# A first selective scan in pieces of 512 columns, and a quarter of each product with C on another engine

## The reference, cut to what matters

```python
def step(state, inp):                      # state: 256 channels x 16 states, for each of 4 sequences
    d, b, c, u = inp                       # one of 256 positions
    dA = jnp.exp(d[..., None] * A)
    state = state * dA + (d * u)[..., None] * b[:, None, :]
    y = jnp.einsum('bdn,bn->bd', state, c)
    return (state, y)
_, ys = jax.lax.scan(step, state0, (dt_t, B_t, C_t, u_t))
```

## Time and profile before

| | us |
|---|---|
| median of 3 timed runs (996.51 to 998.3) | 996.89 |
| span of the profiled execution | 994.6 |
| TensorE busy | 824.6 |
| VectorE busy | 670.0 |
| POOL busy | 419.8 |
| ScalarE busy | 406.1 |
| 32 scans of the first block (L616) | 73.3 |
| 32 products with C (L625) | 38.4 |
| 32 drives (L600) | 75.4 |

### The profile page before, as it was taken

How to read it: one execution, slowest core, us unless ns; L and a number is a source line. 1 busy time by engine, 2 the same in 40 slices (tenths; PEclk the granted TensorE clock), 3 DMA queues, 4 the chain that set the end, 5 groups by cost and what they waited for, 6 DMA issues and landing times.

```text
span 994.6 us, 12963 instructions
## 1 busy us (share of the span) xinstructions
PE 824.6 (83%) x4202; PEld 523.7 (53%) x4202; DVE 670.0 (67%) x1145; ACT 406.1 (41%) x832; POOL 419.8 (42%) x313
## 2 busy tenths in 40 slices
PE   7968898756899888888399779999948988979992
PEld 3323333344677767665377535555525776546651
DVE  5989999697889888889565556778727365412222
ACT  5742333253344444443354725665523432113331
POOL 3036666113575766665169402425501341423331
PEclk9979988756999999999599889999978996979997
DMA  5121214381221221220200121332144010161114
GB/s 216 48 84 67 81 64 181 157 271 52 85 85 50 78 84 42 84 84 0 75 0 1 54 64 50 100 114 76 49 144 135 1 58 7 48 202 48 44 48 153
DMA packets 28531, 81.68 MB, mean 82 GB/s; under 512 B 3360, under 2 KB 17200, under 8 KB 27088
## 3 DMA queue, kind: packets, MB, share of 16 engines
q1 hardware_dynamic: 26080, 73.25, 21.5%
q0 software_dynamic: 2256, 6.18, 1.7%
q10 hardware_dynamic: 144, 1.57, 0.4%
HBM read 65.64 MB, written 17.35 MB: 83 GB/s over the span
## 4 chain that ended last, share of the span: by engine, by line
PE 46%; issue 21%; DVE 17%; POOL 9%; DMA 3%; ACT 2%; SPq 0%; DVEq 0%; POOLq 0%; ACTq 0%
PE ps L522 5%; POOL M L689 5%; PE ps L1357 5%; PE ps L1727 4%; PE ps L1731 4%; PE ps L513 3%; PE ps L1769 3%; PE ps L396 3%; PE ps L911 3%; POOL ZT L994 2%; DVE M L658 2%; PE ps L1376 2%; DVE M L666 2%; PE ps L799 2%; PE ps L1642 1%
## 5 line engine op out<-in xcount | busy, mean ns | idle before, releaser
L799 PE MATMUL ps<-W,F 128*128 128x256 f32 x544 | 151.9, 404 | 34.8 <-DVE W L867 21.7
L799 PEld LDWEIGHTS ps<-W,F 128*128 128x128 f32 x544 | 102.2, 198 | 67.6 <-DVE W L867 40.9
L600 POOL TENSOR_TENSOR M<-M 128x1024 f32<-128x1024 f32 x32 | 75.4, 2356 | 86.1 <-DVE M L474 47.4
L696 POOL TENSOR_TENSOR W<-W,M 128x1024 f32<-128x1024 f32 x32 | 75.4, 2357 | 84.4 <-DVE M L666 84.4
L1798 ACT ACTIVATE N<-ps 128x512 f32<-128x512 f32 x128 | 69.5, 594 | 75.7 <-PE ps L1731 75.7
L831 ACT ACTIVATE F<-ps 128x128 f32<-128x128 f32 x136 | 37.8, 278 | 140.0 <-PE ps L799 140.0
L658 DVE TENSOR_TENSOR_SCAN M<-ps,M 128x512 f32<-128x512 f32 x64 | 78.0, 1219 | 21.5 <-POOL M L689 21.5
L1819 DVE TENSOR_REDUCE W<-ps 128x4 f32<-128x1024 f32 x64 | 78.1, 1221 | 8.9 <-PE ps L1731 5.9
L786 PE MATMUL ps<-W,F 128*128 128x256 f32 x272 | 83.3, 389 | 0.0
L1727 PE MATMUL ps<-M,W 32*128 32x256 f32 x512 | 74.1, 418 | 10.8 <-DVE W L1825 5.7
L616 DVE TENSOR_TENSOR_SCAN M<-ps,M 128x1024 f32<-128x1024 f32 x32 | 73.3, 2291 | 10.3 <-ACT ps L569 10.1
(11 more groups left out here) (281 smaller groups left out, 1708.8 us busy)
## 6 DMA issues: line engine op xcount, KB each, us to landing
M<-dbl_scratch SPq DMA_DIRECT2D x48, 512.0 KB, 3.7
W<-in_gu SPq DMA_DIRECT2D x1, 4800.0 KB, 16.3
W<-in_gu SPq DMA_DIRECT2D x1, 4352.0 KB, 13.9
att_scratch<-W SPq DMA_DIRECT2D x32, 128.0 KB
slot_scratch<-in_slots SPq DMA_DIRECT2D x1, 3999.0 KB, 18.7
M<-slot_scratch SPq DMA_DIRECT2D x3, 1032.0 KB, 9.6
W<-in_gu SPq DMA_DIRECT2D x2, 1536.0 KB, 6.7
W<-in_dn SPq DMA_DIRECT2D x1, 2176.0 KB, 18.6
```

What stands on the lines that cost most here:

```text
L600: nc.gpsimd.tensor_tensor(dBu[:, t, :], du[0][:, t, :], Bb[:, par, :], ALU.mult).then_inc(S("dBu_rdy"), 1)
L696: nc.gpsimd.tensor_tensor(u[1][:, t, :], u[1][:, t, :], hC[:, t, :], ALU.add).then_inc(S("y1_acc"), 1)
L799: last = nc.tensor.matmul(up, ztt[:, par, c, :], gu[:, c, s, :], start=(c == 0), stop=(c == DC - 1))
```

## The change

- `scan` becomes two scans of 512 columns, each with a bank of decays of its own; `decays` writes 510 columns at a time and waits for the scan of that half before. `h_rdy` now counts four a state. ScalarE's loop over the states is written out.
- VectorE's product covers columns 0 to 767 (`OWN`). Columns 768 to 1023 are made by POOL (`weigh_rest`, L611 after) from the state in SBUF and `Cb`, into which SP loads the last 256 columns of C[n], 128 KB over the partitions. The semaphore is `hCp_rdy`.
- POOL's order in the turn of state n: drive (n,0), quarter (n-1,0), drive (n,1), quarter (n-1,1). The wait at the head of a turn is for 32 counts more of `bc0` or `bc1`, 16 from B[n] and 16 from C[n].
- SP loads B[n] and then C[n], the latter when both quarters with C[n-2] are done.
- The scans wait for POOL's quarter as well as for VectorE's own product of the state before, the second half of each sum and each spread wait for the quarters. The other edits adapt counts.

The diff, cut where only counts change:

```diff
--- before.py
+++ after.py
@@ -58,6 +58,7 @@
 SLOTS = SLOT_TILES * P
 ROW = DIM + 2
 RING = 4
+OWN = 768
 SLOT_LOADS = (2, 5, 8, 8, 8)
 LD_W3 = 10 * 16
 ZTT_STEPS = [2 * v for v in TILED_STEPS]
@@ -360,16 +361,24 @@
             for par in range(2):
                 sp.dma_start(Bb[:, par, :], dbl_dram[0][par, :].rearrange("(o n) -> o n", o=1).to_broadcast([P, TOK])
                              ).then_inc(S(f"bc{par}"), 16)
+                sp.dma_start(Cb[:, par, OWN:], dbl_dram[0][par + NSTATE, OWN:].rearrange("(o n) -> o n", o=1)
+                             .to_broadcast([P, TOK - OWN])).then_inc(S(f"bc{par}"), 16)
             with sp.Fori(1, NSTATE // 2) as i:
                 for par in range(2):
                     row = sp.snap(i * 2 + par)
+                    crow = sp.snap(i * 2 + (par + NSTATE))
+                    weighed_before = sp.snap(i * 4 + (2 * par - 2))
                     sp.wait_ge(S("dBu_rdy"), i * 4 + 2 * par - 2)
                     sp.dma_start(Bb[:, par, :], dbl_dram[0][bass.ds(row, 1), :].to_broadcast([P, TOK])
                                  ).then_inc(S(f"bc{par}"), 16)
+                    sp.wait_ge(S("hCp_rdy"), weighed_before)
+                    sp.dma_start(Cb[:, par, OWN:], dbl_dram[0][bass.ds(crow, 1), OWN:].to_broadcast([P, TOK - OWN])
+                                 ).then_inc(S(f"bc{par}"), 16)
 
         def mamba1_sync(sp):
             sp.wait_ge(S("dbl_out"), 32)
             sp.wait_ge(S("dBu_rdy"), 2 * NSTATE)
+            sp.wait_ge(S("hCp_rdy"), 2 * NSTATE)
             for par in range(2):
                 load_rows(sp, 1, par, par)
             with sp.Fori(1, NSTATE // 2) as i:
@@ -508,6 +517,7 @@
             def spread_row(n):
                 if n:
                     pe.wait_ge(S("hC_rdy"), 2 * n)
+                    pe.wait_ge(S("hCp_rdy"), 2 * n)
                 at = DTR + NSTATE + n
                 for half in range(2):
                     last = nc.tensor.matmul(ps[:, 6 + half, :], ident[0:KDBL, at:at + 1].to_broadcast([KDBL, P]),
@@ -519,6 +529,8 @@
                 if n == 0:
                     pe.wait_ge(S("sp_in"), 4)
                 for half in range(2):
+                    if half:
+                        pe.wait_ge(S("hCp_rdy"), n * 2 + t + 1)
                     last = nc.tensor.matmul(ps[:, 2 * t + half, :], ident[:],
                                             hC[:, t, half * HALF:(half + 1) * HALF], start=(n == 0), stop=True,
                                             skip_group_check=True)
@@ -563,18 +575,19 @@
 
             def decays(n, first):
                 for t in range(2):
-                    if not (first and t == 0):
-                        act.wait_ge(S("h_rdy"), n * 2 + t)
-                    scale = Aneg[:, t, n:n + 1] if isinstance(n, int) else Aneg[:, t, bass.ds(n, 1)]
-                    nc.scalar.activation(batches(dAp)[:, :, 1:], batches(delta[0][:, t, :])[:, :, 1:], ACT.Exp,
-                                         scale=scale).then_inc(S("dA_rdy"), 1)
-
-            decays(0, True)
-            with act.Fori(1, NSTATE) as n:
-                decays(n, False)
+                    for half in range(2):
+                        if not (first and t == 0):
+                            act.wait_ge(S("h_rdy"), n * 4 + 2 * t + half - 1)
+                        scale = Aneg[:, t, n:n + 1]
+                        b = slice(2 * half, 2 * half + 2)
+                        nc.scalar.activation(batches(dAp)[:, b, 1:], batches(delta[0][:, t, :])[:, b, 1:], ACT.Exp,
+                                             scale=scale).then_inc(S("dA_rdy"), 1)
+
+            for n in range(NSTATE):
+                decays(n, n == 0)
 
         def mamba_tail_scalar(act, l):
-            act.wait_ge(S("h_rdy") if l == 0 else S("h1_rdy"), 2 * NSTATE * (l + 1))
+            act.wait_ge(S("h_rdy") if l == 0 else S("h1_rdy"), 4 * NSTATE)
             act.wait_ge(S("z_done"), NT * (2 * l + 1))
             for t in range(2):
                 nc.scalar.activation(dA[:, t, :].rearrange("p (b l) -> p b l", b=BATCH), Z[:, t::2, :],
@@ -591,38 +604,52 @@
         def mamba0_gpsimd(pool):
             pool.wait_ge(S("du_done"), 2)
 
+            def weigh_rest(n, par, t):
+                pool.wait_ge(S("h_rdy"), n * 4 + 2 * t + 2)
+                if not (isinstance(n, int) and n == 0):
+                    pool.wait_ge(S("y_acc"), n * 2 + t - 1)
+                nc.gpsimd.tensor_tensor(hC[:, t, OWN:], hst[:, t, OWN:], Cb[:, par, OWN:], ALU.mult).then_inc(S("hCp_rdy"), 1)
+
             def steps(i, first):
                 for par in range(2):
-                    pool.wait_ge(S(f"bc{par}"), 16 + i * 16)
+                    pool.wait_ge(S(f"bc{par}"), 32 + i * 32)
                     for t in range(2):
                         if not (first and par == 0):
-                            pool.wait_ge(S("h_rdy"), i * 4 + 2 * par + t - 1)
+                            pool.wait_ge(S("h_rdy"), i * 8 + 4 * par + 2 * t - 2)
                         nc.gpsimd.tensor_tensor(dBu[:, t, :], du[0][:, t, :], Bb[:, par, :],
                                                 ALU.mult).then_inc(S("dBu_rdy"), 1)
+                        if not (first and par == 0):
+                            weigh_rest(i * 2 + (par - 1), 1 - par, t)
 
             steps(0, True)
             with pool.Fori(1, NSTATE // 2) as i:
                 steps(i, False)
+            for t in range(2):
+                weigh_rest(NSTATE - 1, 1, t)
 
         def mamba0_vector(dve, link):
             softplus_vector(dve, link, 0)
 
             def scan(n, t, first):
                 g = n * 2 + t
-                dve.wait_ge(S("dA_rdy"), g + 1)
-                dve.wait_ge(S("dBu_rdy"), g + 1)
-                if not first:
-                    dve.wait_ge(S("hC_rdy"), g - 1)
-                nc.vector.tensor_tensor_scan(hst[:, t, :], dAp, dBu[:, t, :], 0.0,
-                                             ALU.mult, ALU.add).then_inc(S("h_rdy"), 1)
+                for half in range(2):
+                    at = slice(half * HALF, (half + 1) * HALF)
+                    dve.wait_ge(S("dA_rdy"), 2 * g + half + 1)
+                    if half == 0:
+                        dve.wait_ge(S("dBu_rdy"), g + 1)
+                        if not first:
+                            dve.wait_ge(S("hC_rdy"), g - 1)
+                            dve.wait_ge(S("hCp_rdy"), g - 1)
+                    nc.vector.tensor_tensor_scan(hst[:, t, at], dAp[:, at], dBu[:, t, at], 0.0,
+                                                 ALU.mult, ALU.add).then_inc(S("h_rdy"), 1)
 
             def weigh_states(n, t, first):
                 g = n * 2 + t
-                dve.wait_ge(S("h_rdy"), g + 1)
+                dve.wait_ge(S("h_rdy"), 2 * g + 2)
                 dve.wait_ge(S("cb_rdy"), n + 1)
                 if not first:
                     dve.wait_ge(S("y_acc"), g - 1)
-                nc.vector.tensor_tensor(hC[:, t, :], hst[:, t, :], Cp, ALU.mult).then_inc(S("hC_rdy"), 1)
+                nc.vector.tensor_tensor(hC[:, t, 0:OWN], hst[:, t, 0:OWN], Cp[:, 0:OWN], ALU.mult).then_inc(S("hC_rdy"), 1)
 
             scan(0, 0, True)
             scan(0, 1, True)
...
```

More of the change, by code:

```diff
@@ L661, in mamba1_vector @@
                 if half == 0:
-                    dve.wait_ge(S(f"bc{par}"), 8 * NSTATE + 32 + tile * 32)
+                    dve.wait_ge(S(f"bc{par}"), 16 * NSTATE + 32 + tile * 32)
                     if not start:
@@ L685, in mamba1_drive @@
             if t == 0:
-                pool.wait_ge(S(f"bc{par}"), 8 * NSTATE + 32 + tile * 32)
+                pool.wait_ge(S(f"bc{par}"), 16 * NSTATE + 32 + tile * 32)
             if not (isinstance(tile, int) and tile == 0 and par == 0):
```

## The result

| | before | after |
|---|---|---|
| median of the timed runs, us | 996.7 (995.24 to 998.3) | 1022.41 (1020.67 to 1023.16) |
| span of the profiled execution, us | 994.6 | 1021.4 |
| product (0,1) of the first scan begins, us | 77.43 | 75.49 |
| product (14,1) begins, us | 179.78 | 207.61 |
| a turn of that loop (difference / 14), us | 7.31 | 9.44 |

The changed kernel is slower: ratio 1.0257, 95% interval 1.0225 to 1.0289, 25.7 us between the medians. 1015.3 us was forecast, 18.4 us more than before, with a range of 1006 to 1030.

What follows compares the result with a forecast made beforehand. POOL bounds the loop, waiting openly for C's load: 6.04 + 0.17 + 2.5 + 0.08 = 8.79 us a turn. Time: 994.6 + 18.4 + 2.3 = 1015.3 us, range 1006 to 1030 us.

Steps and rivals of the forecast that it cites:

- POOL bounds the loop through the open load: First scan's loop: C's load is issued after POOL's last quarter and awaited next, so its whole transfer stands open; 8.79 us a turn.
- The predicted signs: Profile of the loop: POOL's t = 0 drives idle about 2.7 us behind the DMA, t = 1 near nothing; VectorE 77% busy.
- rival B: First scan's loop: C's load lands like a row of B, 3.5 us instead of 2.5, giving 1029 us; 12 in 100.
- The sum: First scan's loop: turns of 8.79 us against 7.31 end product (14,1) at 199.4 us, 18.4 us later than before.
- POOL's work: POOL's turn in the loop: two drives of 2.35 us and two quarters of 0.67 us, 6.04 us together.
- The wait: Between POOL's last quarter and next drive: 0.17 us to the load's issue, 2.5 landing, 0.08 to POOL's start.
- The start: Head of the loop: the first half decay takes 0.69 us instead of 1.11, so the first scan begins at 67.3 us.
- The tail: Behind product (14,1): TensorE's last spread, 3.12 us, and three sums, 7.57 us, follow as before; nothing added.
- Scans in halves: VectorE's scans: two of 512 columns cost 2.44 us instead of 2.29, +0.30 a turn, against 0.42 us of waits removed.
- rival A: First scan's loop: the load stays hidden and VectorE bounds at 6.85 us a turn, 988 us, faster; 5 in 100.
- The queue behind the loop: SP's weight loads for the next stage land near 211 us, needed by TensorE at 232; hidden with 21 us of cover.
- Rival C: First scan's loop: TensorE's clock falls and TensorE bounds, 11.6 to 11.7 us a turn, 1056 us; 6 in 100.

Runs made afterwards that it cites:

- the second run: Changed kernel with C's load on its own semaphore, awaited only ahead of the quarter, split at 768, repeated with more rounds: 984.67 us, ratio 0.9872.

## Why the prediction held, and where it was off

**POOL bounds the loop through the open load: shown.** The predicted signs are there. Each drive of t = 0 from turn 2 on is released by the DMA; those of t = 1 follow within 0.1 us; the scans of t = 0 wait 30.8 / 15 = 2.05 us for the quarter (2.0 forecast). Taking the wait off the path, with all else left, turns +26 us into -12. The time grew by 25.7 us where 18.4 were forecast: the range held, as it had been drawn up to rival B, but the middle of the forecast was too low by one term.

**The sum.** Each turn was forecast at 8.79 us and took 9.44; over 14 turns that is 9.1 us too little, and product (14,1) did end 9.1 us later than forecast (208.54 against 199.4). The miss in the time is smaller (7.1), since behind the loop 0.8 us came back and the timed runs lie 1.0 us above the profiled span where 2.3 were added. Term by term:

- POOL's work: 6.04 forecast, 6.02 measured. The quarter took 0.726 us, at the upper bound of 0.73, but consecutive instructions on POOL begin up to 0.05 us before the one ahead has ended by its row, which gives that back.
- The wait: 2.75 forecast, 3.42 measured. **This is the mis-sized term.** The landing was put at 2.5 us from a load of 68.5 KB out of another tensor and was 3.0; from POOL's end to the issue 0.18 (0.17); from the landing to POOL's start 107.49 - 104.34 - 3.0 = 0.15 (0.08). That makes 3.33; the mean is 3.42, since single loads took up to 3.8. The value was chosen by the number of lines and by bytes, and the nearer likeness was the loads of B, which read one row 128 times too: between 3.5 us for 512 KB and the 2.4 us row, a value near 3 would have followed. It is half the way to rival B, which forecast 3.5 and 1029 us. Rival B's thought, that reading one row 128 times costs by the number of reads, is borne out in so far as 8 KB in 128 lines already took 2.5 us; the bytes count too, with 4.0 us at 512 KB, and the run from x leaves open whether it is the one row.
- The start: product (0,1) ended 2.2 us earlier than before (75.49 + 0.93 against 78.64), as in the sum.
- The tail: from the end of product (14,1) to the first instruction behind the last sum 219.28 - 208.54 = 10.7 us, before 191.83 - 180.99 = 10.8. Nothing was added there, rightly.

Product (14,1) ended 27.6 us later than before, the span is 26.8 us longer. The medians differ by 25.7 us; the profiled execution of the changed kernel was the slowest of its four.

**Scans in halves cost less than assumed.** A pair of half scans takes 2.34 us from its start to its end, not 2 x 1.219: the second begins before the first has ended by its row. With it VectorE's own turn is about 6.5 us rather than 6.76, which did not show in the changed kernel, as POOL sets its turn, but it did in the versions with a hidden load: 6.64 against the 6.85 of rival A (and 6.86 in the second run, for its first two turns). For the same reason, and for the longer turn, VectorE was busy for 68% of the loop and not 77%.

**The queue behind the loop: hidden, as forecast.** The second load of weights was issued at 200.3, landed 18.1 us later, and TensorE needed it at 241.3: 23 us of cover (21 forecast).

**Rival A** fell as a forecast, since the load is not hidden as the change has it; as a mechanism it was right, and its 988 us is near what the kernel gives when the wait is moved (984.6). **Rival C** came true in its first half: the granted clock in the loop is 0.76, where it was 0.89 in the loop before, some spreads take 3.8 us and others 1.98, and VectorE's products wait 9.7 us for spreads. It costs next to nothing, because the scan behind such a product waits for POOL anyway. The run with loads from x has a clock of 0.89 and the same 6.02 us beside its wait.

```profile
75.00:195.00 120.00, 93.77 (x170) 33.09 (x168) 89.46 (x86) 38.71 (x57) 84.51 (x57) 0.89 0.28 92
```

The Trainium skill ("DMA: Bandwidth & Descriptors", "Rules for kernel authors") says to issue a DMA early and to wait on its semaphore late. The runs agree, with its price: the same load costs 3.42 us a turn where the wait comes first and nothing where it comes a turn later. The same page's section "Anatomy of one DMA" gives a fixed 2.0 us plus bytes over 436 GB/s for DMAs that GpSimd issues, an estimate of 2.3 us for 128 KB; the prediction took it over for loads that SP issues without saying so. The estimate is met by the load from x (2.3) and missed by the loads of the change (3.0); for these rows the measurement decides.

## What to carry to other kernels

Before an engine's queue is given a wait for a load, look at what released the load's buffer: if it is that engine's own last instruction, the whole transfer stands open, and making it small helps little (2.91 us at 8 KB, 3.42 at 128 KB). Two loads that are needed at different times should not share a semaphore, since the engine then waits for the later one where it needs only the earlier. And when an instruction is moved ahead in a queue to cover such a wait, everything else it waits for moves ahead with it.

## What the runs showed of the hardware that was not expected

- An 8 KB load in 128 lines of 64 bytes takes 2.5 us to land, 64 KB 2.9, 128 KB 3.0 and 512 KB 4.0 us: most of a small load's time does not go by its bytes.
- 128 KB in 128 lines of 1 KB landed in 3.0 us from one row of a scratch that is spread to all partitions, and in 2.3 us from 128 places of an input.
- Two scans of 512 columns in a row take 2.34 us together, only 0.05 more than one of 1024 (2.29), though each alone shows 1.21.
